# Low queries before value parts, places before scores, and a ScalarE copy of the columns beside the rows: one edit in three stages of a two-layer attention and expert kernel

## The chip, the cores and the metric

The kernel runs on one core of one Trainium2 chip. The metric is device microseconds (us) of one execution; lower is better. Five engines work side by side, each through its own list of instructions in order, and wait for each other on counters (semaphores): TensorE (PE in rows; PEld is its weight load), VectorE (DVE), ScalarE (ACT), GpSimd (POOL) and SyncE (SP, which only issues transfers).

## What is computed

Two layers are applied to 2048 tokens of width 256, each a cross attention over 154 context rows and then a mixture of 8 experts of which each token takes 2. Cut to what matters:

```
x = x + attention0(layernorm(x), ctx, ctx, mask)          # 16 heads of 16, softmax(QK/4 masked) V, then wo
x = x + experts0(layernorm(x))                            # top 2 of 8, silu(x wg) * (x wu), then wd; width 1024
x = x + attention1(layernorm(x), ctx, ctx, side inputs)   # one head of 256, softmax(QK/16 + side) V
x = x + experts1(layernorm(x))                            # top 2 of 8, gelu(x W1a) * (x W1b), then W2; width 512
```

In the second mixture an expert takes at most 640 (token, choice) pairs, in token order; what comes later is dropped.

## The kernel before, in words

The 2048 tokens are 16 tiles of 128, in four groups of 4 tiles (g = 0 to 3). Everything that must be nearly exact is held as a high and a low half-precision part: TensorE multiplies both, and ScalarE usually makes the high part (a cast) and VectorE the low part (value minus high part). The order on each engine is written out by hand, in one function per engine; nothing is scheduled by a program.

**Start of layer one.** TensorE projects keys (`project_keys`) and values (`project_values`, into PSUM banks 6 and 7), turns the first group's normalised tokens and projects its queries. VectorE then makes the key parts (`key_parts`), four `value_parts` (head and remainder parts of the values, for two batches; they release banks 6 and 7 with the signal `kv_done`), the moments and the inverse root of group 1 (`moments`, `scale_and_shift`, whose `a0_nb` lets ScalarE normalise that group), and the low part of the first queries (`q_low(0)`). TensorE's `score_max(0, 1)` waits for that low part. Twelve `score_max` steps fill two pairs of banks in turn and twelve `maximum` steps on VectorE empty them; the query projection of group 1 (`project_q("a0", 1, ...)`) stands among them on TensorE, after step 5, and writes to banks 6 and 7. `negate(0)` and `turn_max(0)` then release the exponentials of group 0.

**Attention of layer two.** Per group g, VectorE adds the attended values to x and takes the routing logits (`attended_rows`), sends the moments to GpSimd (`moments_for_gpsimd`), makes the low part of the next softmax weights (`low_weights`, line 1872), picks the two experts (`choose`), scales the logit difference (`gate_difference`), takes the attention scores of group g + 2 from PSUM and their maxima (`logits(g + 2)`, lines 1854 to 1867), makes the low part of the normalised rows (`low_rows`, line 1901) and computes the place of each row in the experts' lists (`place`, lines 1654 to 1674, signal `r1_slot`). `place(g)` needs the running count from TensorE (`route_positions(g)`, signal `r1_pos_ps`). TensorE's hand-written order there is: weigh the values of group g + 1, count the positions of group g, turn the weights of group g + 2, score the tokens of group g + 3. ScalarE takes the exponentials of group g + 2 as soon as `logits(g + 2)` has given the maxima. GpSimd scatters the rows to DRAM: per group eight indirect transfers (line 631), and before the fifth of them the inverse root of the next group (`scale_and_shift`, lines 608 to 620), which waits for that group's moments.

**The mixtures** (`experts`, once per layer). The sorted rows are read in blocks of 256; a token row of 520 half-precision numbers is high part, low part and, as four 32-bit numbers, the token, two gate weights and the first expert (`TOKEN, SECOND, GAIN, FIRST`). There is one input buffer, `x_raw`. Per block g, TensorE multiplies by the gate and up weights, turns block g + 1 (`turn_block`, line 933, which waits for its load), and multiplies by the down weights; ScalarE applies silu or gelu (line 1267) and casts (line 1271), then issues the load of block g + 2 (`load`, line 1253), then writes the scaled result (line 1280); VectorE multiplies, makes low parts, and in `turned(g + 1)` (lines 1783 to 1790) copies the turned block and works out each row's gate weight from the four trailing numbers, which it reads in `x_raw`, signal `r_carried`; GpSimd adds the result to the sums in DRAM (line 575). ScalarE waits, before the load of block g + 2, for the turning of block g + 1 and for its `r_carried`:

```
act.wait_ge(S(r + "_xbT_ps"), g + 3)
act.wait_ge(S(r + "_carried"), g + 2)
load(g + 2)
split(pairs)
act.wait_ge(S(r + "_down"), g + 2)
wait_counted(act, S(r + "_added"), g + 1)
```

The new weights of a coming expert are converted inside its first block (`high_part` line 1129 on ScalarE, `low_part_of` line 1405 on VectorE); `_added` says that GpSimd's addition of the block before has landed.

Of the kernel before, what the change touches and what calls it, by code (L numbers as in the profile page):

```python
# [16 lines left out]
ALU = mybir.AluOpType  # L17
# [54 lines left out]
def two_layers(nc, a, out):  # L72
    with ExitStack() as ctx:
# [181 lines left out]
        share = sb("share", [P, 2])  # L255
        expert_of = sb("expert_of", [P, AHEAD])
# [235 lines left out]
        def _(pool):  # L492
# [130 lines left out]
            def scatter(l, g):  # L623
                r = l.r
                pool.wait_ge(S(r + "_xp"), g + 1)
                pool.wait_ge(S(r + "_slot"), g + 1)
                for t in range(GT):
                    if l.n == 1 and t == 2 and g + 1 < NG:
                        scale_and_shift("r1", g + 1)
                    for k in range(TOP):  # L630
                        pool.indirect_dma_start(  # L631
                            out=rows, out_offset=bass.IndirectOffsetOnAxis(ap=slot_s[:, g * GT + t, k:k + 1], axis=0),
                            in_=beside_row[g % l.held][:, t, :], in_offset=None, bounds_check=E * REGION - 1,
                            oob_is_err=False).then_inc(S(f"{r}_scattered{g % 2}"), 16)
# [48 lines left out]
        def _(pe):  # L683
# [180 lines left out]
            for n in range(12):  # L864
                score_max(0, n)
                if n == 2:
                    pe.wait_ge(S("k_split"), B)
                    turn("a0", 1, xln, 4, done=3)
                if n == 5:
                    pe.wait_ge(S("kv_done"), 1)  # L870
                    project_q("a0", 1, w_sb["wq"], q_bank(1))
# [237 lines left out]
        def _(act):  # L1109
# [133 lines left out]
            def experts(l):  # L1243
# [10 lines left out]

                def one_block(g, coming=None):
# [6 lines left out]
                    for j in range(pairs + 1):  # L1262
# [5 lines left out]
                        if j:  # L1268
# [3 lines left out]
                            split(j - 1)  # L1272
                    act.wait_ge(S(r + "_xbT_ps"), g + 3)
                    act.wait_ge(S(r + "_carried"), g + 2)
# [25 lines left out]
                load(0)  # L1300
                act.wait_ge(S(r + "_padded"), 16 * (E - 1))
                act.wait_ge(S(r + "_xbT_ps"), 2)
                act.wait_ge(S(r + "_carried"), 1)
# [36 lines left out]
            def tokens_normalised(g):  # L1340

                if g:
                    act.wait_ge(S("r1_xp"), g)
                normalise("r1", g, g + 1)
                act.wait_ge(S("r1_ln"), GT * (g + 1))
                act.copy(xps[g][:, :, 0:D], xln[:, :, :]).then_inc(S("r1_xhi"), 1)
# [14 lines left out]
            gates(L[1], 0)  # L1361
# [4 lines left out]
            gates(L[1], 1)  # L1366
# [3 lines left out]
            gates(L[1], 2)  # L1370
            tokens_normalised(3)
            gates(L[1], 3)
# [4 lines left out]
        def _(dve):  # L1377
# [138 lines left out]
            dve.wait_ge(S("kv_ps"), 2)  # L1516
            for n in range(4):
                value_parts(n // 2, n % 2)
# [198 lines left out]
            q_low(0)  # L1717
            for n in range(12):
                maximum(0, n)
            negate(0)  # L1720
# [54 lines left out]
            def experts(l):  # L1775
# [5 lines left out]
                def turned(g):  # L1781
# [4 lines left out]
                    dve.scalar_tensor_tensor(share[:, :], raw[:, :, FIRST], expert_of[:, bass.ds(g, 1)], raw[:, :, GAIN], ALU.is_equal,  # L1786
                                             ALU.mult).then_inc(S(r + "_share"), 1)
                    dve.tensor_copy(own[:, :, 1].bitcast(I32), raw[:, :, TOKEN].bitcast(I32))
                    wait_counted(dve, S(r + "_share"), g + 2)
                    dve.tensor_tensor(own[:, :, 0], share[:, :], raw[:, :, SECOND], ALU.add).then_inc(S(r + "_carried"), 1)  # L1790

                raw = x_raw[:, :, :].bitcast(F32)
# [105 lines left out]
            def low_rows(g):  # L1898

                dve.wait_ge(S("r1_xhi"), g + 1)  # L1900
                dve.tensor_tensor(xps[g][:, :, D:2 * D], xln[:, :, :], xps[g][:, :, 0:D], ALU.subtract).then_inc(S("r1_xp"), 1)
# [14 lines left out]
            for g in range(NG):  # L1916
# [7 lines left out]
                gate_difference(g)  # L1924
                if g + 2 < NG:
                    logits(g + 2)
                low_rows(g)
                place(L[1], g)
# [47 lines left out]
```

## Time and profile before

| | us |
|---|---|
| median of 3 runs (lowest, highest) | 886.07 (883.26, 892.51) |
| profiled execution, own time | 890.67 |
| its span, first to last instruction | 889.0 |
| mean granted TensorE clock, of full speed | 0.889 |

| stage in the profiled span, us | from | to |
|---|---|---|
| start of layer one, up to the first exponentials | 0 | 54 |
| rest of attention and routing, layer one | 54 | 293 |
| mixture of layer one | 293 | 601 |
| attention and routing, layer two | 601 | 709 |
| mixture of layer two | 709 | 889 |

A row of a timeline reads: start in us, duration in us, engine, line, operation, output<-inputs, shapes, count (x4 is four in a row, with their time in sum), and in brackets how long the engine had been idle and what ended that. A row of stretches gives busy time and count of each engine, then the granted clock, the busy share of the DMA engines and GB/s.

### The profile page before, as it was taken

Reading aid. Unit: us, or ns where it says so; the run is one execution under the profiler, and the core shown is the slowest. Engines: PE = TensorE matmul, PEld = TensorE weight load, DVE = VectorE, ACT = ScalarE, POOL = GpSimd, SP = SyncE. Lnnn points to the kernel's source line nnn. Section 1 sums busy time; section 2 is a strip of 40 time slices with the busy share of each in tenths; the row PEclk is TensorE's granted clock in tenths of the full one; section 3 lists DMA queues with packets and bytes.
Section 4 is the critical chain, followed back from the end, with each engine's and each line's share of the span. In section 5 each row is a group of like instructions: output and inputs, shape, how many; then the busy total and the mean of one; then the engine's idle time right before and its main releaser. Section 6 shows DMA issues by size and latency. Waiting matters only on the chain.

```text
span 889.0 us, 19049 instructions
## 1 busy us (share of the span) xinstructions
PE 700.3 (79%) x6278; PEld 550.1 (62%) x6278; DVE 547.8 (62%) x1322; ACT 403.1 (45%) x720; POOL 302.8 (34%) x306
## 2 busy tenths in 40 slices
PE   5476796989564799999999899996862098898981
PEld 4232454555354688888897798895531087777771
DVE  7768576887836545647556656547696446566441
ACT  1135466576513434646545555442552044546331
POOL 7505301416337422222121131232167414334342
PEclk9689799989776799999999999997875599999996
DMA  4562300601524542536344643425022555464332
GB/s 140 118 141 51 59 2 24 180 24 49 153 81 151 185 129 36 165 51 171 78 126 98 170 112 101 107 39 179 25 101 95 174 170 131 115 147 114 63 55 40
DMA packets 68418, 92.24 MB, mean 104 GB/s; under 512 B 14442, under 2 KB 54435, under 8 KB 68348
## 3 DMA queue, kind: packets, MB, share of 16 engines
q1 hardware_dynamic: 41788, 63.37, 24.1%
q0 software_dynamic: 14592, 16.24, 10.6%
q10 hardware_dynamic: 11968, 11.72, 5.3%
q8 instruction: 42, 0.69, 0.3%
q14 instruction: 28, 0.23, 0.1%
HBM read 64.21 MB, written 29.87 MB: 106 GB/s over the span
## 4 chain that ended last, share of the span: by engine, by line
PE 48%; DVE 18%; issue 11%; ACT 9%; POOL 5%; DMA 5%; ACTq 2%; another core or an unknown queue 1%; DVEq 0%; POOLq 0%; SPq 0%
PE ps L685 45%; POOL rows L631 3%; DVE probs L1726 3%; DVE mx L1591 2%; DMA out_x<-keys,row_to 2%; DVE keys L1804 2%; DMA probs<-rows 2%; ACT probs L1189 1%; ACT probs L1271 1%; ACT expo L1186 1%; DVE keys L1783 1%; ACT probs L1267 1%; PE ps L933 1%; DVE stats L1383 1%; ACTq L1252 1%
## 5 line engine op out<-in xcount | busy, mean ns | idle before, releaser
L1804 DVE TENSOR_TENSOR keys<-probs,ps 128x512 f32<-128x512 f32 x122 | 82.8, 687 | 177.3 <-ACT probs L1267 86.3
L685 PE MATMUL ps<-keys,slot 128*128 128x256 f16 (+1 forms) x1440 | 146.5, 263 | 5.4 <-DVE keys L1783 2.7
L685 PE MATMUL ps<-keys,probs 128*128 128x256 f16 (+1 forms) x1488 | 139.5, 255 | 5.1 <-DVE probs L1405 3.7
L685 PEld LDWEIGHTS ps<-keys,slot 128*128 128x128 f16 x1440 | 127.8, 99 | 22.8 <-issue 5.4
L685 PEld LDWEIGHTS ps<-keys,probs 128*128 128x128 f16 x1488 | 124.2, 98 | 19.0 <-issue 7.2
L575 POOL DMA_INDIRECT attended<-keys,row_to x42 | 67.2, 1601 | 166.0 <-ACT keys L1280 142.2
L1267 ACT ACTIVATE probs<-ps 128x512 f32<-128x512 f32 x122 | 71.4, 598 | 65.9 <-PE ps L685 63.7
L1280 ACT ACTIVATE keys<-ps,carried 128x256 f32<-128x256 f32 x80 | 33.5, 470 | 117.9 <-POOLq L580 41.6
L1809 DVE TENSOR_TENSOR probs<-keys,probs 128x512 f16<-128x512 f32 x122 | 83.3, 688 | 3.6 <-ACT probs L1271 1.9
L1271 ACT CAST probs<-keys 128x512 f16<-128x512 f32 x122 | 74.8, 614 | 22.0 <-DVE keys L1804 21.9
L1726 DVE TENSOR_TENSOR probs<-expo,probs 128x512 f16<-128x512 f32 x80 | 61.1, 775 | 34.1 <-ACT probs L1189 28.2
L685 PE MATMUL ps<-slot,probs 128*128 128x256 f16 x636 | 74.8, 273 | 3.7 <-ACT probs L1271 3.0
L685 PE MATMUL ps<-probs 128*128 128x256 f16 x612 | 72.4, 273 | 4.8 <-ACT probs L1271 4.4
L575 POOL DMA_INDIRECT out_x<-keys,row_to x38 | 58.8, 1548 | 45.6 <-ACT keys L1280 36.6
L1186 ACT ACTIVATE expo<-ps 128x512 f32<-128x512 f32 x80 | 48.2, 602 | 52.8 <-PE ps L685 46.9
L685 PEld LDWEIGHTS ps<-slot,probs 128*128 128x128 f16 x636 | 60.0, 98 | 14.4 <-ACT probs L1271 4.2
L685 PEld LDWEIGHTS ps<-probs 128*128 128x128 f16 x612 | 57.5, 98 | 15.8 <-ACT probs L1271 4.5
L571 POOL COPY row_to<-carried 128x2 int32 x40 | 10.1, 252 | 139.0 <-issue 45.5
L933 PE MATMUL ps<-identh,probs 128*128 128x128 f16 x336 | 26.5, 224 | 36.5 <-DMA probs<-rows 36.5
L685 PE MATMUL ps<-penalties,identb 128*128 128x462 bf16 x96 | 34.8, 363 | 22.2 <-DVE queries L1569 9.4
L1189 ACT CAST probs<-expo 128x512 f16<-128x512 f32 x80 | 49.0, 619 | 0.0
L1405 DVE TENSOR_TENSOR probs<-inbox,probs 128x1024 f16<-128x1024 f32 x36 | 43.6, 1221 | 6.1 <-ACT probs L1129 6.0
(285 smaller groups left out, 1145.7 us busy)
## 6 DMA issues: line engine op xcount, KB each, us to landing
inbox<-in_W SPq DMA_DIRECT2D x24, 512.0 KB, 3.9
probs<-rows ACTq DMA_DIRECT2D x44, 260.0 KB
inbox<-in_wg SPq DMA_DIRECT2D x16, 512.0 KB, 5.2
inbox<-in_wu SPq DMA_DIRECT2D x16, 512.0 KB, 3.7
inbox<-in_wd SPq DMA_DIRECT2D x16, 512.0 KB, 4.2
rows<-zeros SPq DMA_DIRECT2D x16, 260.0 KB
x<-in_x SPq DMA_DIRECT2D x4, 512.0 KB, 6.1
q_out<-queries SPq DMA_DIRECT2D x8, 256.0 KB, 2.1
```

What stands on the lines that cost most here:

```text
L575: pool.indirect_dma_start(out=l.sums, out_offset=bass.IndirectOffsetOnAxis(ap=row_to[:, hf:hf + 1], axis=0), in_=yb[:, hf, :], in_offset=N ...
L685: return pe.matmul(o, l, r, start=start, stop=stop, **kw)
L933: last = pe.transpose(psh[:, 6, part * BLK + hf * P:part * BLK + (hf + 1) * P], x_raw[:, hf, part * P:(part + 1) * P], identh[:, :])
L1186: act.activation(e_ring[:, u % 4, :], ps[:, 4 + u % 2, :], ACT.Exp, scale=float(DK) ** -0.5).then_inc(S("a0_exp"), 1)
L1189: act.copy(p_hi[:, u - 1, :], e_ring[:, (u - 1) % 4, :]).then_inc(S("a0_phi"), 1)
L1267: act.activation(s_act[:, j % 2, :], ps[:, 2 * (j % 2), :], l.act).then_inc(S(r + "_s"), 1)
L1271: act.copy(h_hi[:, 2 * j - 2:2 * j, :].rearrange("p c t -> p (c t)"), h32[:, (j - 1) % 2, :]).then_inc(S(r + "_hh"), 1)
L1280: ins = act.activation(yb[:, hf, :], ps[:, 4 + hf, 0:D], ACT.Identity, scale=carried[:, bass.ds(g, 1), hf, 0:1].rearrange("p b d -> p (b d)"))
L1405: dve.tensor_tensor(w[:, 1, at:at + CH], stage[:, n % STAGES, :], w[:, 0, at:at + CH], ALU.subtract).then_inc(S(f"w_ready{l.n}"), 1)
L1726: dve.tensor_tensor(p_lo[:, u, :], e_ring[:, u % 4, :], p_hi[:, u, :], ALU.subtract).then_inc(S("a0_plo"), 1)
L1804: dve.tensor_tensor(h32[:, j % 2, :], s_act[:, j % 2, :], ps[:, 2 * (j % 2) + 1, :], ALU.mult).then_inc(S(r + "_h32"), 1)
L1809: dve.tensor_tensor(h_lo[:, 2 * j - 2:2 * j, :].rearrange("p c t -> p (c t)"), h32[:, (j - 1) % 2, :], h_hi[:, 2 * j - 2:2 * j, :].rearran ...
```

## The change

It has three parts. (1) At the start of layer one, `q_low(0)` comes before the value parts; the four value parts stand now before maximum 0 and behind maxima 2, 5 and 7, and TensorE's projection of group 1 moves from behind step 5 to behind step 8. (2) In layer two, ScalarE and VectorE make each group's rows in two halves of two tiles, with `gates` between ScalarE's halves, GpSimd waits for a half before the transfers that read it, and `place` and `low_rows` come before `logits(g + 2)`. (3) In both mixtures ScalarE copies the four trailing numbers of block g + 1 to a small tile, `beside_now`, behind its casts of block g; VectorE reads them there, and the load of block g + 2 waits for this copy instead of `r_carried`. The copy itself waits until VectorE has used the block before. Added or moved lines:

```
 def scatter(l, g):
-    pool.wait_ge(S(r + "_xp"), g + 1)
+    if l.n == 0:
+        pool.wait_ge(S(r + "_xp"), g + 1)
     pool.wait_ge(S(r + "_slot"), g + 1)
     for t in range(GT):
+        if l.n == 1 and t % 2 == 0:
+            pool.wait_ge(S(r + "_xp"), 2 * g + t // 2 + 1)
...
-                if n == 5:
+                if n == 8:
                     pe.wait_ge(S("kv_done"), 1)
                     project_q("a0", 1, w_sb["wq"], q_bank(1))
...
+                def keep_beside(g):
+
+                    act.wait_ge(S(r + "_xraw"), g * 16 + 16)
+                    act.wait_ge(S(r + "_carried"), g)
+                    act.copy(beside_now[:, :, :], x_raw[:, :, :].bitcast(F32)[:, :, D:D + 4]).then_inc(S(r + "_beside"), 1)
...
+                    keep_beside(g + 1)
                     act.wait_ge(S(r + "_xbT_ps"), g + 3)
-                    act.wait_ge(S(r + "_carried"), g + 2)
+                    act.wait_ge(S(r + "_beside"), g + 2)
                     load(g + 2)
...
             def tokens_normalised(g):
-                if g:
-                    act.wait_ge(S("r1_xp"), g)
-                normalise("r1", g, g + 1)
-                act.wait_ge(S("r1_ln"), GT * (g + 1))
-                act.copy(xps[g][:, :, 0:D], xln[:, :, :]).then_inc(S("r1_xhi"), 1)
+                for j in range(2):
+                    if g:
+                        act.wait_ge(S("r1_xp"), 2 * g - 1 + j)
+                    half = slice(2 * j, 2 * j + 2)
+                    normalise("r1", g, g + 1, (2 * j, 2 * j + 1))
+                    act.wait_ge(S("r1_ln"), GT * g + 2 * j + 2)
+                    act.copy(xps[g][:, half, 0:D], xln[:, half, :]).then_inc(S("r1_xhi"), 1)
+                    if j == 0:
+                        gates(L[1], g)
...
             key_parts(1)
-            dve.wait_ge(S("kv_ps"), 2)
-            for n in range(4):
-                value_parts(n // 2, n % 2)
             dve.wait_ge(S("ld_x1"), 16)
...
             q_low(0)
+            dve.wait_ge(S("kv_ps"), 2)
+            value_parts(0, 0)
             for n in range(12):
                 maximum(0, n)
+                if n in (2, 5, 7):
+                    part = (2, 5, 7).index(n) + 1
+                    value_parts(part // 2, part % 2)
...
             def low_rows(g):
-                dve.wait_ge(S("r1_xhi"), g + 1)
-                dve.tensor_tensor(xps[g][:, :, D:2 * D], xln[:, :, :], xps[g][:, :, 0:D], ALU.subtract).then_inc(S("r1_xp"), 1)
+                for j in range(2):
+                    half = slice(2 * j, 2 * j + 2)
+                    dve.wait_ge(S("r1_xhi"), 2 * g + j + 1)
+                    dve.tensor_tensor(xps[g][:, half, D:2 * D], xln[:, half, :], xps[g][:, half, 0:D], ALU.subtract).then_inc(S("r1_xp"), 1)
...
                 gate_difference(g)
+                place(L[1], g)
+                low_rows(g)
                 if g + 2 < NG:
                     logits(g + 2)
-                low_rows(g)
-                place(L[1], g)
```

In `turned`, `raw[:, :, FIRST]` and its like become `beside_now[:, :, FIRST - D]`, behind a wait for `r_beside`. The order on the engines, at the two places that matter most (line numbers of the changed kernel run 4 to 17 higher). VectorE in the attention of layer two, group 0, before; `cumb` ends `choose(0)`, `dv` is `gate_difference`, `lg_x` to `mx` is `logits(2)`, `xp<-xln,xp` is `low_rows`, `ohp` begins `place` (its middle left out: from `posk` to `slot_s`), `rd` begins `attended_rows(1)`:

```order
L1646 TENSOR_TENSOR cumb<-cumb,gsum 128x8
L1618 TENSOR_TENSOR dv<-dv,ry_r 128x4
L1854 COPY lg_x<-ps 128x32
L1858 SCALAR_TENSOR_TENSOR expo<-ps,ry_a,keys 128x154 x4
L1865 TENSOR_REDUCE mx<-expo 128x4
L1867 TENSOR_SCALAR mx<-mx 128x4
L1901 TENSOR_TENSOR xp<-xln,xp 128x4x256
L1654 TENSOR_TENSOR ohp<-oh,ps 128x64
L1656 TENSOR_REDUCE posk<-ohp 128x8
...
L1674 TENSOR_TENSOR xp<-dn,xp 128x4
L1878 RECIPROCAL rd<-den 128x4
```

The same place now:

```order
L1656 TENSOR_TENSOR cumb<-cumb,gsum 128x8
L1628 TENSOR_TENSOR dv<-dv,ry_r 128x4
L1664 TENSOR_TENSOR ohp<-oh,ps 128x64
L1666 TENSOR_REDUCE posk<-ohp 128x8
...
L1684 TENSOR_TENSOR xp<-dn,xp 128x4
L1918 TENSOR_TENSOR xp<-xln,xp 128x2x256 x2
L1869 COPY lg_x<-ps 128x32
L1873 SCALAR_TENSOR_TENSOR expo<-ps,ry_a,keys 128x154 x4
L1880 TENSOR_REDUCE mx<-expo 128x4
L1882 TENSOR_SCALAR mx<-mx 128x4
L1893 RECIPROCAL rd<-den 128x4
```

The four steps of `logits(2)` moved from the third row to behind the places and the low rows, which are two halves now.

ScalarE at the end of a block of the mixture, before (`probs<-keys` is the last cast, `TENSOR_LOAD` and `DMA` are the load of block g + 2, `keys<-ps,carried` the scaled result):

```order
L1271 CAST probs<-keys 128x512
L1129 CAST probs<-inbox 128x1024 x2
L1273 REGISTER_ALU
L1274 REGISTER_ALU
L1252 ISA
L1252 TENSOR_LOAD table
L1252 ISA x2
L1253 ISA
L1253 DMA probs<-rows 128x2x260
```

and now:

```order
L1133 CAST probs<-inbox 128x1024 x2
L1261 ISA
L1263 COPY beside_now<-probs 128x8
L1284 REGISTER_ALU
L1285 REGISTER_ALU
L1256 ISA
L1256 TENSOR_LOAD table
L1256 ISA x2
L1257 ISA
L1257 DMA probs<-rows 128x2x260
```

One small copy stands now between the casts and the load; on VectorE nothing moved there.

## Rows read from the trace of the kernel before

**Rows 1.** Stretches (us; PE, PEld, DVE, ACT, POOL busy): mixture one, scatter, mixture two
```profile
307.00:601.00 294.00, 286.59 (x2955) 257.36 (x2953) 172.99 (x285) 148.67 (x244) 68.66 (x59) 0.99 0.44 108
650.00:705.00 55.00, 16.27 (x79) 7.02 (x77) 36.68 (x175) 14.93 (x31) 40.50 (x44) 0.53 0.35 124
719.00:872.00 153.00, 136.72 (x1391) 114.75 (x1388) 87.25 (x168) 72.27 (x127) 60.37 (x53) 1.00 0.50 108
```

**Rows 2.** Timeline of VectorE at the start of layer one
```profile
22.28 0.41 DVE L1493 TENSOR_TENSOR slot<-ps,b_bv 128x256 f32<-128x256 f32 x1
...
28.70 1.40 DVE L1383 BATCH_NORM_STATS2 stats<-x 128x6 f32<-128x256 f32 x4
...
32.80 1.40 DVE L1569 SCALAR_TENSOR_TENSOR queries<-ps,b_bq,queries 128x512 f16<-128x512 f32 x2
...
45.95 2.15 DVE L1591 TENSOR_REDUCE mx<-ps 128x6 f32<-128x924 f32 x2 [3.25 <-PE ps L685]
...
52.33 0.23 DVE L1603 SCALAR_TENSOR_TENSOR nm<-mx,nm 128x64 bf16<-128x64 f32 x1
```

**Rows 3.** Timeline of TensorE at six places of the kernel
```profile
41.50 3.64 PE L685 MATMUL ps<-xT,w_wq 128*128 128x512 f32 x8
...
402.27 5.42 PE L685 MATMUL ps<-keys,slot 128*128 128x256 f16 x48 [1.27 <-DVE keys L1804]
...
616.84 4.69 PE L685 MATMUL ps<-heads,xT 128*128 128x162 f32 x16 [1.10 <-ACT xT L1323]
...
646.33 0.19 PE L685 MATMUL ps<-selb,earlier 128*128 128x32 bf16 x1
...
653.78 6.23 PE L685 MATMUL ps<-probs,queries 128*128 128x264 f16 x24 [2.92 <-DVE queries L1873]
...
661.38 1.12 PE L1058 MATMUL ps<-ident,expo 128*128 128x128 f32 x4 [1.13 <-ACT expo L1329]
```

**Rows 4.** Timeline of ScalarE at a loop's end in layer one, in attention, in mixture two
```profile
397.44 0.84 ACT L1280 ACTIVATE keys<-ps,carried 128x256 f32<-128x256 f32 x2 [3.31 <-issue]
399.43 1.28 ACT L1267 ACT_TABLE_LOAD   x1 [1.14 <-issue]
...
645.77 0.41 ACT L1329 ACTIVATE expo<-expo,mx 128x154 f32<-128x154 f32 x1
...
756.41 0.38 ACTq L1253 DMA_DIRECT2D probs<-rows  x1
757.10 0.84 ACT L1280 ACTIVATE keys<-ps,carried 128x256 f32<-128x256 f32 x2 [3.32 <-POOLq L580]
```

**Rows 5.** Timeline of VectorE in attention of layer two and in mixture two
```profile
642.93 0.18 DVE L1854 COPY lg_x<-ps 128x32 f32<-128x32 f32 x1
...
645.80 1.23 DVE L1901 TENSOR_TENSOR xp<-xln,xp 128x1024 f16<-128x1024 f32 x1 [0.31 <-ACT xp L1346]
646.94 0.21 DVE L1654 TENSOR_TENSOR ohp<-oh,ps 128x64 f32<-128x64 f32 x1
...
648.20 0.17 DVE L1674 TENSOR_TENSOR xp<-dn,xp 128x4 f32<-128x4 f32 x1
...
664.57 0.69 DVE L1872 TENSOR_TENSOR queries<-ps,queries 128x512 f16<-128x512 f32 x1
...
755.47 0.16 DVE L1790 TENSOR_TENSOR carried<-share,probs 128x2 f32 x1 [0.15 <-issue]
```

**Rows 6.** Timeline of GpSimd, scatter of layer two
```profile
649.32 1.11 POOL L631 DMA_INDIRECT rows<-xp,slot_s  x1 [7.80 <-DVE xp L1674]
...
663.28 0.98 POOL L631 DMA_INDIRECT rows<-penalties,slot_s  x1 [0.30 <-issue]
...
668.17 0.23 POOL L608 TENSOR_SCALAR var_p<-mv_r 128x4 f32<-128x4 f32 x1
```

**Rows 7.** Waits from 705 to 889 us: total, times, longest
```profile
ACT keys L1280 <- POOLq L580: 41.6, 11, 4.4
...
PE ps L933 <- DMA probs<-rows: 25.4, 8, 19.2
```

More of the change, by code:

```diff
@@ L255, in two_layers @@
         share = sb("share", [P, 2])
+        beside_now = sb("beside_now", [P, 2, 4])
         expert_of = sb("expert_of", [P, AHEAD])
@@ L1300, in experts @@
                 load(0)
+                act.wait_ge(S(r + "_xraw"), 16)
+                act.copy(beside_now[:, :, :], x_raw[:, :, :].bitcast(F32)[:, :, D:D + 4]).then_inc(S(r + "_beside"), 1)
                 act.wait_ge(S(r + "_padded"), 16 * (E - 1))
                 act.wait_ge(S(r + "_xbT_ps"), 2)
-                act.wait_ge(S(r + "_carried"), 1)
+                act.wait_ge(S(r + "_beside"), 1)
                 load(1)
@@ L1360, in _ @@
             tokens_normalised(0)
-            gates(L[1], 0)
             exponentials(2)
@@ L1365, in _ @@
             tokens_normalised(1)
-            gates(L[1], 1)
             exponentials(3)
@@ L1369, in _ @@
             tokens_normalised(2)
-            gates(L[1], 2)
             tokens_normalised(3)
-            gates(L[1], 3)
             experts(L[1])
@@ L1785, in turned @@
                     wait_counted(dve, S(r + "_share"), g + 1)
-                    dve.scalar_tensor_tensor(share[:, :], raw[:, :, FIRST], expert_of[:, bass.ds(g, 1)], raw[:, :, GAIN], ALU.is_equal,
+                    dve.wait_ge(S(r + "_beside"), g + 1)
+                    dve.scalar_tensor_tensor(share[:, :], beside_now[:, :, FIRST - D], expert_of[:, bass.ds(g, 1)], beside_now[:, :, GAIN - D], ALU.is_equal,
                                              ALU.mult).then_inc(S(r + "_share"), 1)
-                    dve.tensor_copy(own[:, :, 1].bitcast(I32), raw[:, :, TOKEN].bitcast(I32))
+                    dve.tensor_copy(own[:, :, 1].bitcast(I32), beside_now[:, :, TOKEN - D].bitcast(I32))
                     wait_counted(dve, S(r + "_share"), g + 2)
-                    dve.tensor_tensor(own[:, :, 0], share[:, :], raw[:, :, SECOND], ALU.add).then_inc(S(r + "_carried"), 1)
-                raw = x_raw[:, :, :].bitcast(F32)
+                    dve.tensor_tensor(own[:, :, 0], share[:, :], beside_now[:, :, SECOND - D], ALU.add).then_inc(S(r + "_carried"), 1)
                 def low_part(e, slot, n):
```

## The prediction

> **What bounds the kernel now.** I read the stretches first, to see which engine fills which stage, then the timelines of the three places that the change touches, then the list of waits. The two mixtures are TensorE's: it is busy for 286.6 of 294 us in the one and 136.7 of 153 in the other [rows 1]. So a wait there is worth only what TensorE loses to it. In the attention of layer two the picture is another: from 650 to 705 us TensorE is busy for 16 of 55 us, at a granted clock of 0.53. The reader is to see GpSimd's timeline there [rows 6]: from its first scatter at 649.32 on, each step follows on the last with "issue" (0.30) before it, to the last at about 702. The stage ends with GpSimd, and its reserve is small. At 663.28 it starts group 1 and at 668.17 the root for group 2. Whatever delivers late to these two is paid in full. The start of layer one is a chain over VectorE and TensorE: value parts from 22.28, moments from 28.70, the low queries at 32.80, the maxima, and the last negated maximum ends at 52.56 [rows 2].
>
> **Part 1, start of layer one.** The value parts take 28.70 - 22.28 = 6.4 us, the moments and the root 32.80 - 28.70 = 4.1, the low queries 1.4 [rows 2]. The low queries now end at 22.3 + 4.1 + 1.4 = 27.8 instead of 34.2, 6.4 us sooner. But the 6.4 us of value parts are only moved, among the maxima. A maximum takes 2.15 / 2 = 1.08; nine of them (0 to 8) and the four parts are 9.7 + 6.4 = 16.1, so VectorE is through maximum 8 at about 43.9, and the last value part ends one maximum before, at 42.8. TensorE's projection of group 1 (3.64 [rows 3]) waits for exactly that part: 42.8 + 3.6 = 46.4. Behind it stand the scores 9 to 11 (under 1 us each), then three maxima (3.2) and the negation (0.5): 46.4 + 0.8 + 3.7 = 50.9 against 52.6. What hid the projection before was in part VectorE's idle 3.25 [rows 2]; that idle time comes back behind the last value part. Gain 1.7 us. It goes on to the end, as everything later hangs on it. Bounds: a gain of 2.5 if the scores run close, a loss of 1.9 if the projection runs at half the clock after TensorE's waits (3.64 more).
>
> **Part 2, attention of layer two.** Before, VectorE had finished choosing group 0 at 642.93 and went straight into the scores of group 2, 642.93 to 645.49 (the row after waited 0.31 before 645.80), so 2.56 us [rows 5]. Now `place(0)` stands there, and its positions are counted by TensorE only at 646.33 [rows 3], behind the weighing of group 1, which nothing in the change moves. VectorE stands still for 3.7 us, until 646.6. That is an added wait on an engine with the next group's work queued behind it.
>
> Step by step: place 1.43 (646.94 to 648.37), low rows 1.23, say 1.3 in two halves, scores 2.56 [rows 5]: the scores of group 2 end at 646.6 + 1.4 + 1.3 + 2.6 = 651.9 instead of 645.5. Queued behind them: the exponentials (four at 0.41, 1.7 [rows 4]) to 653.7; the turning of the weights and ScalarE's copies, from the turning at 661.38 to the low weights at 664.57 being 3.2 [rows 3, 5], so low weights at 657.0, done at 658.3 (2 x 0.69, less overlap). TensorE meanwhile turns (2.2) and scores group 3, 4.7 at the lower clock [rows 3], to 660.6. The weighing of group 2 took 6.2 at the lower clock; it lies between half of that, 3.1, and 6.2. I take 3.6, since TensorE will have worked for 6.8 us without a pause. So positions of group 1 at 664.5, its place done at 665.9, its first half of low rows at 666.6: GpSimd starts group 1 3.3 us late (663.28).
>
> Then it repeats. Low rows end at 667.2, scores of group 3 at 669.8, exponentials 671.5, low weights 674.7 to 676.0, and only then, in VectorE's order for group 2, the moments (1.4 and 0.4): 677.8. GpSimd wants them after half a group, at 666.6 + 4.9 (663.28 to 668.17) = 671.5; before, it took them at 668.17 [rows 6]. Loss 9.6 us, say 9.5. From there on nothing is late: group 2's place is done at about 683.5, GpSimd comes for it at 686.5. For groups 2 and 3 no scores stand in the way.
>
> The halves gain almost nothing. GpSimd's first scatter waited for the place (`slot`, 648.37), not for the low rows at 647.0; now the place is done at 648.0 and the first half at 648.7. I count 0.
> Bounds of part 2: with both turnings, the scoring and the weighing at the full clock about 5 us less, +5; with the weighing at the lower clock 2.6 more, +12.
>
> **The clock.** The trace shows the lower of the two levels (1.2 against 2.4 GHz) in this stretch, 0.53 granted, after waits of 2.9 us [rows 1, 3]. The Trainium skill ("TensorE: Matmul & The Clock Gate", What's actually happening) says that the slow state is the default and activity releases it. By that rule the longer pauses keep TensorE slow; taken for the weighing too, part 2 costs 12 and not 9.5.
>
> **Part 3, the mixtures.** ScalarE's load of block g + 2 waited for VectorE's `r_carried`, ending at 755.63; the load went out 0.78 later, at 756.41, and the result 0.69 after that, at 757.10, after 3.32 us of idle time, so since 753.8 [rows 4, 5]. Now the load follows on the casts: 753.8, a copy of 8 columns (under the 0.41 of a 154-column step [rows 4]; I take 0.2), 0.8: 754.8, so 1.6 us sooner. Where weights are converted ScalarE is busy until shortly before, and I count about 0.3 there. VectorE's own steps cost the same.
>
> In mixture one TensorE has few gaps. At the ends of ScalarE's loop a table load follows on the late result (397.44 after 3.31 idle, 399.43), and TensorE waits 1.27 at 402.27 [rows 3, 4]; a second such wait, of 1.27 too, stands at 477.32. The result comes 1.4 sooner, bound now by the down product, so both gaps go: 2.5. The last block's result is 1.4 sooner as well, and layer two starts on it: 1.2 after what VectorE's own moments keep back. Sum 3.7; bounds 1.5 and 4.5. The copy itself is hidden under ScalarE's idle 3.3 us per block; uncovered it would be 0.2 per block.
>
> In mixture two TensorE waited for loads for 25.4 us in 8 waits, 19.2 of it the first [rows 7]. The other seven are 6.2 us, under 1.8 each, so 1.6 sooner nearly removes them. Behind each stands the wait for ScalarE's cast, which follows on the result before and moves forward too, but by less where weights are converted. I take three quarters, 4.7; bounds 0.6 and 7.
>
> **Sum.** 890.67 (span 889.0 and 1.7 around it) - 1.7 + 9.5 - 3.7 - 4.7 = 890.1, 0.6 less. The profiled run lies 4.6 above the median; taken from the median, 886.07 - 0.6 = 885.5.
>
> **Rivals.**
> *The moved place costs nothing.* If VectorE's 3.7 us lie beside GpSimd's scatter, only the gains remain, 10.1: 876. For it: VectorE is busy for only 37 of 55 us there [rows 1]. Against it: the exponentials, the weighing and the moments all hang on its order, with GpSimd 1 us behind them.
> *The additions hold mixture two.* ScalarE's result waits for GpSimd's addition of the block before; eleven such waits make 41.6 us [rows 7]. If they are what they seem, an earlier load moves nothing, the gain there is 0.6, and the sum is +3.5, slower: 889.6. It decides where an addition lands later than the load is out. Against it: the result at 757.10 follows on the load by just 0.69, so GpSimd was there already.
> *The slow clock through all of layer two*: part 2 costs 12, sum +1.9: 888.
> *Both, and a slow projection at the start* (3.6 more): +9.6, 895.7.
>
> **Chances.** Forecast 0.45, clock 0.18, additions 0.14, place for nothing 0.15, all against 0.08. The measurement tells about 1% from no change, 8.9 us: faster by more 0.16, within 0.75, slower by more 0.09. The range, 875.5 to 893, takes in the bounds of parts 2 and 3 against each other and the case in which the place costs nothing, and leaves out the last case.
>
> **What would show it.** Right: the first low-query step at about 26.4 and the last negation at 51; VectorE idle 3.6 us before the first `ohp` of layer two, GpSimd waiting once for group 1's place and some 6 us for group 2's moments; the gaps at 402 and 477 gone; 1 to 2 us left of the seven waits for loads. Wrong: GpSimd's scatter still without waits, or the results of mixture two at their old distance.

## The result and the profile after

The changed kernel takes 893.12 us (median of 20 runs, 886.34 to 900.88), the kernel before 883.73 (20 runs). The ratio is 1.0091, 95% interval 1.0075 to 1.0108: some 8 us slower, just outside the range I gave and on its slow side. The two medians lie 9.4 us apart; the ratio counts the fast runs alone (one of the 20 was slow), and its interval, 6.6 to 9.5 us, holds that too. I had forecast no change.

The two profiled executions hide this: after took 890.15 us, 3 below its median, and before 890.67, 7 above its own; the spans are 888.4 and 889.0. What makes up the difference is mostly the stretch up to the first turned block of mixture one, which ends anywhere from 285 to 294 us in the seventeen profiles of this study, with no relation to what was changed that I can see. So I compare stages, not spans. The stages go from the first turned block of mixture one to layer two's first turned token ("mixture one"), from there to the first turned block of mixture two ("attention two"), and to the end ("mixture two"):

| us | up to mixture one | mixture one | attention two | mixture two |
|---|---|---|---|---|
| before | 293.4 | 320.4 | 95.4 | 179.8 |
| after | 288.4 | 312.2 | 102.5 | 185.3 |
| after, a second profile | 291.2 | 314.3 | 99.4 | 183.7 |

Mixture one is shorter, attention two longer, and mixture two, from which I expected 4.7 us less, is 3.9 to 5.5 us longer. The stretches of after that answer to [rows 1] (mixture one, scatter, mixture two; columns as there):

```profile
307.00:596.00 289.00, 284.06 (x2941) 256.16 (x2938) 170.62 (x286) 150.48 (x266) 72.88 (x62) 1.00 0.44 107
640.00:700.00 60.00, 17.54 (x96) 10.32 (x96) 38.59 (x183) 18.57 (x44) 36.40 (x43) 0.56 0.33 116
713.00:872.00 159.00, 137.98 (x1400) 116.23 (x1396) 88.55 (x169) 74.89 (x146) 62.88 (x53) 0.99 0.48 105
```

TensorE's work is the same, but mixture two now holds 138.0 us of it in 159 instead of 136.7 in 153: it waits more. For what, the waits of after from 705 to 889 us say (engine, line, what it waited for, total, times, longest), beside [rows 7]:

```profile
ACT keys L1291 <- POOLq L581: 48.5, 12, 5.4
...
POOL row_to L572 <- DMA out_x<-keys,row_to: 40.6, 11, 5.0
```

and over 705 to 887 us:

```profile
PE ps L937 <- DMA probs<-rows: 2.7, 2, 1.6
```

In the kernel before, over 705 to 889 us, the middle one was:

```profile
POOL row_to L571 <- DMA out_x<-keys,row_to: 32.3, 11, 3.2
```

TensorE's waits for loads behind the first, 6.2 us before, are down to 2.7, as forecast. But GpSimd's eleven waits until an addition has landed grew from 2.9 to 3.7 us each, and the waits of ScalarE's results for that from 41.6 us in 11 to 48.5 in 12. In the chain that ended last the additions' landing now has 8% of the span, before 2%.

In attention two the marks that I had named are there, and two more short waits of GpSimd. VectorE stands still before the first place, GpSimd waits 1.57 us for the moments of group 1, 1.56 for the rows of group 1 and 5.6 for the moments of group 2 (timelines of after, VectorE and GpSimd):

```profile
634.78 0.22 DVE L1664 TENSOR_TENSOR ohp<-oh,ps 128x64 f32<-128x64 f32 x1 [3.98 <-PE ps L689]
```

```profile
637.76 1.11 POOL L635 DMA_INDIRECT rows<-xp,slot_s  x1 [8.46 <-DVE xp L1918]
...
644.30 0.23 POOL L609 TENSOR_SCALAR var_p<-mv_r 128x4 f32<-128x4 f32 x1 [1.57 <-DVE mv_r L1408]
...
653.55 0.97 POOL L635 DMA_INDIRECT rows<-penalties,slot_s  x1 [1.56 <-DVE penalties L1918]
...
663.98 0.23 POOL L609 TENSOR_SCALAR var_p<-mv_r 128x4 f32<-128x4 f32 x1 [5.61 <-DVE mv_r L1408]
```

At the start of layer one the low queries come at 26.95 us, 5.9 sooner than in [rows 2], and yet the negation is late. VectorE (with GpSimd's clearing of a query tile beside it) and TensorE in after:

```profile
26.95 1.40 DVE L1579 SCALAR_TENSOR_TENSOR queries<-ps,b_bq,queries 128x512 f16<-128x512 f32 x2
...
33.26 0.20 DVE L1512 COPY v_rem<-quad_of 128x16 f16<-128x16 f16 x1
...
41.74 1.27 DVE L1512 COPY v_rem<-quad_of 128x16 f16<-128x16 f16 x1
...
50.07 2.15 DVE L1601 TENSOR_REDUCE mx<-ps 128x6 f32<-128x924 f32 x2 [5.50 <-PE ps L689]
...
53.25 0.22 DVE L1613 SCALAR_TENSOR_TENSOR nm<-mx,nm 128x64 bf16<-128x64 f32 x1
```

```profile
41.15 1.80 POOL L553 MEMSET qs<- 128x2048 f32 x1
```

```profile
43.85 5.40 PE L689 MATMUL ps<-xT,w_wq 128*128 128x512 f32 x8 [3.10 <-DVE v_rem L1516]
```

Two things are not as reckoned: the copy of 16 columns takes 1.27 us where its twin takes 0.20, and the projection 5.40 where it took 3.64 [rows 3].

### The profile page after: what moved, and what is told of

It is laid out like the page before. It is cut to its first block, busy times and chain, and to the rows that moved or that the text cites. A ratio compares the mean times of both kernels' runs of the same rounds, so it can differ in the third digit from the quotient of the medians.

```text
span 888.4 us, 19136 instructions
## 1 busy us (share of the span) xinstructions
PE 699.8 (79%) x6266; PEld 555.9 (63%) x6278; DVE 551.2 (62%) x1326; ACT 408.1 (46%) x766; POOL 305.1 (34%) x306
## 4 chain that ended last, share of the span: by engine, by line
PE 48%; DVE 17%; issue 11%; DMA 10%; ACT 7%; POOL 4%; POOLq 1%; ACTq 1%; DVEq 0%
PE ps L689 45%; DMA out_x<-keys,row_to 8%; DVE probs L1741 3%; DVE mx L1601 2%; POOL rows L635 2%; ACT probs L1193 2%; PE ps L937 1%; ACT expo L1190 1%; DVE stats L1396 1%; POOL out_x L576 1%; ACT probs L1133 1%; DMA probs<-rows 1%; ACT keys L1291 1%; DVE expo L1873 1%; DVE queries L1579 0%
## 5 line engine op out<-in xcount | busy, mean ns | idle before, releaser
L689 PE MATMUL ps<-keys,probs 128*128 128x256 f16 (+1 forms) x1488 | 137.6, 254 | 4.6 <-DVE probs L1418 3.5
L572 POOL COPY row_to<-carried 128x2 int32 x40 | 14.0, 350 | 149.1 <-issue 48.6
```

Of the source, the lines that this page charges most:

```text
L689: return pe.matmul(o, l, r, start=start, stop=stop, **kw)
```

## The experiments

Each kernel was timed against the kernel before on its own chip, so ratios compare and medians don't.

### Each part alone

The first of these has the diff's edits to `q_low`, `value_parts` and `project_q`; the second those to `scatter`, `tokens_normalised`, `low_rows` and `place`; the third those to `keep_beside`, `load` and `turned`.

> The kernel before with part 1 alone (low queries ahead of the value parts, projection of group 1 behind step 8). Theory: the profile after shows the projection at 5.40 us instead of 3.64 and the last negation 0.9 us later, so part 1 is a small loss: ratio 1.000 to 1.002, some +1 us, the last negation at about 53.4. Rival (my prediction's term): a gain of 1.7 us, ratio 0.998, last negation at about 51.

> The kernel before with part 2 alone (row halves and places ahead of the scores in layer two). Theory: the chain over GpSimd's waits costs what the profile after shows, +7 us (stage from the first turn of layer two to the first turn of mixture two 102.5 instead of 95.4 us), ratio 1.007 to 1.009. Rival: the later scatter also takes the whole loss of mixture two with it (by another phase of the weight loads), then +12 us, ratio 1.014, and mixture two at 185 instead of 180 us with the load where it was.

> The kernel before with part 3 alone, in both mixtures (ScalarE's copy, the load waits for it). Theory: the earlier load falls on GpSimd's additions in mixture two, which land 4.2 us after their issue instead of 3.0; mixture two 185 us instead of 180 (+5), mixture one 4 to 8 us shorter, so between -3 and +1 us, ratio 0.997 to 1.001. Rival (the prediction's term): both mixtures gain, -8 us, ratio 0.991, the profile's loss in mixture two coming from elsewhere.

| | ratio (interval) | mixture one | attention two | mixture two |
|---|---|---|---|---|
| part 1 alone | 1.0012 (0.9995 to 1.0029) | 320.9 | 97.1 | 181.3 |
| part 2 alone | 1.0039 (1.0015 to 1.0062) | 320.8 | 100.8 | 179.9 |
| part 3 alone | 1.0004 (0.9975 to 1.0034) | 315.5 | 95.9 | 184.3 |

The stage effects stay with their parts. Part 2 leaves mixture two alone, so that rival falls, but it costs 5.4 us in its stage and not the 7 that I had read off the profile after. Part 3 gains 4.9 us in mixture one and loses 4.5 in mixture two, to no net effect. Part 1 ends its negation at 53.0 and doesn't gain.

### The parts together again

> The changed kernel as it is, on the chip that runs the three below, so that the parts can be added up against it. On another chip the three parts alone came to 1.0012, 1.0039 and 1.0004. If the parts add (theory), their sum is 1.0055; if the earlier load and the later scatter hurt each other (rival), the whole is at 1.008 or more, as in the first measurement (1.0091), and its mixture two is over 1 us longer than with part 3 alone (184.3).

1.0074 (1.0047 to 1.0102). The interval holds both the product of the three parts, 1.0055, and the rival's 1.008, so the ratio doesn't decide. Mixture two is at 183.7, not longer than with part 3 alone, so I see no interaction.

### Part 3 in mixture one alone

```
-                    act.wait_ge(S(r + "_carried"), g + 2)
+                    if l.n == 0:
+                        keep_beside(g + 1)
+                    act.wait_ge(S(r + ("_beside" if l.n == 0 else "_carried")), g + 2)
```

> Part 3 in the first mixture alone; mixture two as before. Theory: in mixture one TensorE sets the end and additions have slack (GpSimd waits for results 130 us there), so the 4.9 us of the profile with part 3 alone stay: ratio 0.993 to 0.996, mixture two at 180 us. Rival: the 4.9 us are chance between profiles and the ratio is 0.998 to 1.002.

0.9946 (0.9924 to 0.9967): faster, with mixture one at 315.0 us and mixture two at 179.4. TensorE's waits there from 287.9 to 603 us:

```profile
PE ps L934 <- issue: 10.7, 1, 10.7
PE ps L1040 <- DMA x<-attended: 6.1, 1, 6.1
PE ps L686 <- DVE probs L1417: 3.5, 1, 3.5
PE ps L686 <- DVE keys L1795: 0.9, 1, 0.9
```

In the kernel before, from 293 to 614 us, the same list was:

```profile
PE ps L933 <- DMA probs<-rows: 11.2, 1, 11.2
PE ps L1039 <- DMA x<-attended: 7.6, 1, 7.6
PE ps L685 <- DVE probs L1405: 3.7, 1, 3.7
PE ps L685 <- DVE keys L1804: 2.5, 2, 1.3
PE ps L685 <- ACT probs L1271: 1.0, 5, 0.2
PE ps L685 <- DVE keys L1783: 0.9, 1, 0.9
```

The two gaps of 1.27 are gone (2.5), and the last wait fell from 7.6 to 6.1: together 4.0. The five short waits for casts (1.0) are no part of the gain, though they are missing here: three other kernels with the copy have them, and four without it don't. The stage is 315.1 us long in the mean of the eight profiles with the copy and 319.9 in the nine without, 4.8 less, but the two groups touch (312.2 to 316.8, and 316.8 to 322.7). TensorE's idle time in the stage tells them apart: 10.3 to 11.8 us with the copy, 14.6 to 16.4 without, 4.5 less in the mean.

### When the load goes out in mixture two

Three kernels move only that. The first two are part 3 alone, but in layer two with

```
+                    if l.n == 1:
+                        act.wait_ge(S(r + "_down"), g + 2)
                     load(g + 2)
```

or with `load(g + 2)` behind `wait_counted(act, S(r + "_added"), g + 1)`. The third is the kernel before with a second load of the same size, into a tile `dump` that nothing reads, issued by ScalarE behind its casts (and behind the landing of the `dump` load before).

> Part 3 in both mixtures, but in layer two the load of block g + 2 waits for the down product of block g too (about 0.7 to 1 us later than with part 3 alone, and still ahead of ScalarE's wait for the addition, so no result waits for the load to be issued). Theory (load and addition share the DMA engines): GpSimd's eleven waits for landing fall from 3.65 us each towards 2.95, and mixture two from 184.3 towards 180 to 182. Rival (the ring is longer for another reason, such as ScalarE's order): mixture two stays at 184 and the waits at 3.6.

> As the run with part 3 alone, but in layer two the load of block g + 2 goes out behind ScalarE's wait for the addition of the block before, so that it does not run while that addition lands. Theory (the load and the additions share the DMA engines): additions land as in the kernel before, about 3 us after their issue, and mixture two is back at 179 to 181 us, 4 to 6 us less than with part 3 alone. Rival (not the load's time but something else of the change holds the ring): the landings stay long and mixture two at 185 us, within 1 us of part 3 alone; second rival: the later load brings TensorE's waits for loads back and costs as much as it gives, mixture two at 183 or more with short landings.

> The kernel before, and in layer two ScalarE issues, behind its casts, a second load of the same size (block g again) into a tile that nobody reads; the real load stays where it was. Theory (a load that runs while an addition lands makes it land later): GpSimd's waits for landing rise from 2.95 to 3.6 us or more each, though no data waits for this load, and mixture two gets 4 to 8 us longer, part of that ScalarE's time to issue it. Rival (transfers don't meet; the early load hurts by another order of waits): the landings stay at 2.9 to 3.1 us, and mixture two gets longer by the issue alone, up to 0.7 us in each of the six blocks that convert weights.

| | ratio (interval) | landing, us each | mixture two |
|---|---|---|---|
| before | 1 | 2.94 | 179.8 |
| part 3 alone | 1.0004 (0.9975 to 1.0034) | 3.65 | 184.3 |
| load behind the down product | 0.9959 (0.9940 to 0.9979) | 3.14 | 179.7 |
| load behind the wait for the addition | 1.0081 (1.0052 to 1.0111) | 3.12 | 192.4 |
| before, with a second load | 1.0109 (1.0086 to 1.0132) | 3.40 | 189.7 |

The landing column is the wait row divided by its eleven waits; for part 3 alone, for the load behind the down product, and for the second load (705 to 887 us):

```profile
POOL row_to L572 <- DMA out_x<-keys,row_to: 40.1, 11, 4.2
```

```profile
POOL row_to L572 <- DMA out_x<-keys,row_to: 34.5, 11, 4.4
```

```profile
POOL row_to L572 <- DMA out_x<-keys,row_to: 37.4, 11, 3.9
```

What costs sits at the results of the blocks of 128 rows, whose casts are through early (an expert's last block, of half the width). At five of the six, GpSimd's waits are 2.77 to 3.12 us before, 3.75 to 4.24 with part 3 alone (5.3 us more in sum, of 7.8 in all eleven) and 2.77 to 2.89 with the load behind the down product; at the sixth they are 2.96, 3.23 and 2.89. In that last kernel the first, third and fifth of the eleven waits stay long (3.94, 4.36 and 3.36), and yet mixture two is as short as before; these three are the only ones beside which packets of a weight load run. ScalarE and GpSimd at such a result with part 3 alone:

```profile
733.07 0.39 ACTq L1254 DMA_DIRECT2D probs<-rows  x1
737.06 0.84 ACT L1288 ACTIVATE keys<-ps,carried 128x256 f32<-128x256 f32 x2 [4.96 <-POOLq L581]
```

```profile
732.10 1.54 POOL L576 DMA_INDIRECT out_x<-keys,row_to  x1 [0.30 <-issue]
737.47 0.19 POOL L572 COPY row_to<-carried 128x2 int32 x1 [3.83 <-DMA out_x<-keys,row_to]
```

and with the load behind the down product:

```profile
728.30 0.39 ACTq L1254 DMA_DIRECT2D probs<-rows  x1
730.20 0.84 ACT L1291 ACTIVATE keys<-ps,carried 128x256 f32<-128x256 f32 x2 [3.94 <-POOLq L581]
```

```profile
726.27 1.54 POOL L576 DMA_INDIRECT out_x<-keys,row_to  x1 [0.30 <-issue]
730.61 0.19 POOL L572 COPY row_to<-carried 128x2 int32 x1 [2.81 <-DMA out_x<-keys,row_to]
```

In the first, the load goes out 4.0 us ahead of the result, while GpSimd is still issuing the second half of the addition (732.10 to 733.64); the addition lands 1.0 us later than in the second, where the load goes out 1.9 us ahead of the result, 0.5 us after GpSimd has issued the second half. The second load, whose data nothing uses, lengthens the landings too, from 2.94 to 3.40 us on average (3.6 or more were expected; mixture two grew by more than the 4 to 8 expected). So it is the load's traffic, and not another order of waits, that makes additions land later.

The kept traces also hold start, size and queue of every single packet, which the rows above don't list. They show how. With part 3 alone, at each of those five, 143 to 194 of the load's 256 packets (1040 bytes each) start ahead of the first 1 KB packet of the addition's second half, which starts 1.5 to 1.8 us after GpSimd has issued it. In the kernel before, and with the load behind the down product, none does, and that packet starts after 0.6 us. The second half queues behind the load. The Trainium skill ("DMA: Bandwidth & Descriptors", Queues, rings and completion order) says that each DMA engine takes turns between the queues that have work for it and finishes a whole packet, typically 9 to 17 descriptors, before it switches. By that rule a load would pass in one piece: its 256 entries of the trace are 16 for each of 16 engines, an estimate, as the trace names no engine. The order in the trace agrees with it; that it is the reason isn't shown.

How much of the 9.9 us that the second load adds to mixture two is landing, and how much ScalarE's time to issue it, stays open. With the load behind the wait for the addition, additions land in 3.12 us, but every result then waits until the load is issued, TensorE waits for loads again (14.3 us in 11 waits), and it is the slowest of the mixtures. So the second rival of that run was right. The right place lies between, and the kernel before already had its load there.

### The result in halves

```
-                    wait_counted(pool, S(r + "_y"), g + 2)
                     for hf in range(2):
+                        wait_counted(pool, S(r + "_y"), g * 2 + (2 + hf))
```

with ScalarE signalling `_y` after each half.

> The kernel before, with one difference: ScalarE signals each half of the scaled result, and GpSimd issues the addition of the first half on that signal, 0.42 us sooner than behind both. Theory (the ring result, addition, landed, result sets mixture two): each ring of 16 full blocks gets 0.4 us shorter, and mixture two 3 to 6 us, ratio 0.994 to 0.997. Rival (TensorE sets mixture two, the ring only looks late): under 1 us, ratio 0.999 to 1.001.

1.0009 (0.9991 to 1.0026): nothing, the rival's number, and in the full blocks for its reason. In eleven of nineteen blocks GpSimd did use the earlier signal: from the start of the result to the addition it is 1.35 us where it was 1.72. Mixture two is no shorter for it. Before (its result is the last row of [rows 4]), and then with halves (ScalarE, GpSimd):

```profile
758.82 1.55 POOL L575 DMA_INDIRECT out_x<-keys,row_to  x1 [1.51 <-ACT keys L1280]
```

```profile
749.43 0.84 ACT L1280 ACTIVATE keys<-ps,carried 128x256 f32<-128x256 f32 x2 [3.32 <-POOLq L580]
...
750.79 1.55 POOL L575 DMA_INDIRECT out_x<-keys,row_to  x1 [1.27 <-ACT keys L1280]
```

At the other eight, those of blocks of 128 rows among them, the gain is 0.1 us or less, as the addition there follows on GpSimd's own small copy, and that on the landing. Before, and then with halves:

```profile
740.17 0.19 POOL L571 COPY row_to<-carried 128x2 int32 x1 [2.77 <-DMA out_x<-keys,row_to]
741.49 1.55 POOL L575 DMA_INDIRECT out_x<-keys,row_to  x1 [1.14 <-ACT keys L1280]
```

```profile
732.49 0.18 POOL L571 COPY row_to<-carried 128x2 int32 x1 [2.82 <-DMA out_x<-keys,row_to]
733.72 1.55 POOL L575 DMA_INDIRECT out_x<-keys,row_to  x1 [1.04 <-ACT keys L1280]
```

From copy to addition it is 1.32 us the one time and 1.23 the other. So in a full block the ring has time to spare, and in a block of 128 rows it is GpSimd and the landing, with ScalarE's wait of 4 us as its shadow. That fits with a later landing being paid, at the blocks of 128 rows, and an earlier result bringing nothing.

### Part 2 taken apart

Halves alone is part 2 without the move of `place` and `low_rows`. The other is part 2 with `route_positions(L[1], 0)` ahead of `weigh_tokens(1)`.

> Only the row halves of layer two (ScalarE, VectorE and GpSimd's two waits), with places and low rows behind the scores as in the kernel before. Theory: the halves are worth nothing and the moved places are all of part 2's cost: ratio 0.999 to 1.001, stage from the first turn of layer two to the first of mixture two at 95 to 96 us. Rival: the halves themselves cost (twice the instructions on VectorE and ScalarE), ratio 1.002 to 1.004 and a stage of 98.

> Part 2 alone, but TensorE counts the positions of group 0 ahead of weighing group 1 (in PSUM bank 4, which is free there) and not behind it. Theory (the moved place costs because it waits for positions that stand behind the weighing on TensorE): VectorE's idle time before the first place falls from 3.66 us to under 1, GpSimd's first scatter and everything behind it comes 3 us sooner, its waits for group 1 (2.35) stay, and of the 5 to 6 us that part 2 adds to the stage 2 to 3 are left (98 instead of 100.8 us; ratio 1.000 to 1.002 against 1.0039). Rival (the scores of group 2 are late by place and low rows anyway, whatever the wait): the stage stays at 100 to 101 us.

Halves alone: 0.9997 (0.9974 to 1.0021), attention two at 95.5 us. So the halves are free within the interval, and the moved places are the cost. Positions first: 1.0057 (1.0030 to 1.0083), attention two at 99.6. The wait is gone and the loss is not. VectorE and GpSimd of that run:

```profile
640.47 0.22 DVE L1658 TENSOR_TENSOR ohp<-oh,ps 128x64 f32<-128x64 f32 x1 [0.39 <-PE ps L688]
...
659.28 0.22 DVE L1658 TENSOR_TENSOR ohp<-oh,ps 128x64 f32<-128x64 f32 x1 [4.01 <-PE ps L688]
```

```profile
644.29 1.11 POOL L634 DMA_INDIRECT rows<-xp,slot_s  x1 [5.72 <-DVE xp L1907]
...
662.17 0.97 POOL L634 DMA_INDIRECT rows<-penalties,slot_s  x1 [3.65 <-DVE penalties L1907]
...
672.61 0.23 POOL L608 TENSOR_SCALAR var_p<-mv_r 128x4 f32<-128x4 f32 x1 [5.63 <-DVE mv_r L1399]
```

GpSimd's waits are 3.65 and 5.63 instead of 2.35 and 5.62 with part 2 alone. The theory of this run is mostly wrong: 1.2 us of the stage came back, not 2 to 3 (the ratio is no smaller than part 2's, as this profile is also 2 to 3 us longer in the two mixtures, which it doesn't touch). The order itself costs: the scores of group 2 start 33.4 us into the stage, against 35.7 with part 2 alone and 29.4 before, so that 4.0 of the 6.3 us stay although the first wait is gone. That much the rival had right. With the place ahead, the scores of group 3 hang on the positions of group 1, these stand behind the weighing of group 2, and that hangs on the scores of group 2: a ring. From the scores of group 2 to those of group 3 it takes 17.9 us here and 16.6 with part 2 alone, against 13.6 in the kernel before and 13.96 from one group's first scatter to the next in [rows 6]. The scores in their old place didn't hang on the positions. That the ring sets these times is read from the order; no run opened it.

### Part 1 taken apart

> Part 1 alone, but with TensorE's projection of group 1 behind step 11 instead of 8. Theory: what cost part 1 its gain is the projection in the middle of the scores, 3.1 us of TensorE idle and 5.3 us of projection while VectorE sits idle for 5.4; behind the last score it lies beside the last three maxima. Last negation at about 48 instead of 52.8, the first exponential group 4 us sooner, and if that goes on to the end, ratio 0.995 to 0.997 (part 1 alone: 1.0012). Rival: the time is given back in the attention of layer one, where TensorE and VectorE are filled anyway, ratio 0.999 to 1.001 with the negation still early.

> Part 1 alone, with GpSimd's clearing of the second query tile (1.80 us, at 40.8) held back until the last value part is done. Theory (VectorE's copy v_rem<-quad_of, 1.27 to 1.66 us instead of 0.20 in three profiles with part 1, is held by that clearing, since it ends each time 0.06 us behind it): the copy takes 0.19 to 0.20 us and the last value part ends 1.1 us sooner, at about 42.4. Rival (the copy is slow for another reason, its place behind the maxima for one): it stays over 1 us. The whole time is no test, 1 us is too little.

The projection behind step 11: 0.9994 (0.9972 to 1.0016). The negation starts at 48.38, 4 us sooner, but TensorE's next step now waits behind the projection, and the first scores of group 0 start at 52.53 instead of 53.88: 1.35 us, too little to measure. (In the ten profiles with the old start they come at 53.0 to 55.0, 54.1 in the mean.)

The clearing held back behind the last value part (a single run, for its timeline). VectorE, GpSimd and TensorE:

```profile
41.73 0.19 DVE L1501 COPY v_rem<-quad_of 128x16 f16<-128x16 f16 x1
...
50.47 0.22 DVE L1602 SCALAR_TENSOR_TENSOR nm<-mx,nm 128x64 bf16<-128x64 f32 x1
```

```profile
42.78 1.80 POOL L554 MEMSET qs<- 128x2048 f32 x1 [1.74 <-DVE v_rem L1505]
```

```profile
42.77 3.70 PE L687 MATMUL ps<-xT,w_wq 128*128 128x512 f32 x8 [2.02 <-DVE v_rem L1505]
```

The copy takes 0.19 us, the projection starts at 42.77 and takes 3.70, and the negation is through at 50.7. The last run below repeats all three. The kernel before already showed the clash, in a row I hadn't read:

```profile
23.03 1.84 POOL L552 MEMSET slot<- 128x2048 f32 x1
```

```profile
24.42 0.51 DVE L1499 COPY v_rem<-quad_of 128x16 f16<-128x16 f16 x1
27.80 0.19 DVE L1499 COPY v_rem<-quad_of 128x16 f16<-128x16 f16 x1
```

The clearing ends at 24.87 and the copy that meets it at 24.93; in after they end at 42.95 and 43.01. The Trainium skill ("SBUF — State Buffer", SBUF: two separate sides) says that VectorE and GpSimd share a pair of memory ports, which whichever starts first holds for its whole instruction while the other stands. It limits this to some VectorE instructions, such as a copy in a mode that uses both ports. Both pairs of rows agree, with 0.06 us between the ends; in which mode the copy ran, no row says.

### The parts that pay, together

> The parts that should pay, together: part 1 with the projection behind step 11, and part 3 in mixture one alone; layer two as before. Part 3 in mixture one alone gave 0.9946. Theory: with the 4 us of the start 0.990 to 0.992. Rival (the start's gain is given back): 0.994 to 0.996.

> Part 1 with GpSimd's second clearing behind the last value part, and part 3 in mixture one alone; attention and mixture of layer two as before. Theory: the first scores of group 0 start at about 51.9 instead of 53.9 (2.0 us), mixture one is 4.8 us shorter, mixture two stays at 179 to 181: together 6.8 of 885, ratio 0.992. Rival (the start's gain does not reach the end, as the 1.35 us with the projection behind step 11 did not show): 0.9946, as with part 3 in mixture one alone.

0.9926 (0.9898 to 0.9955) with the projection behind step 11, 0.9940 (0.9912 to 0.9969) with the mended start. Both beat the kernel before, by 0.6 to 0.7%. Neither is told apart from part 3 in mixture one alone, 0.9946, so that the start's 1.4 to 2 us reach the end isn't shown.

## Why the prediction was wrong

Taking for each stage the mean of the profiles with and without its part, the terms are +0.6, +5.5, -4.8 and +4.2: 5.5 us more, where I had 0.6 less. The second measurement, 1.0074, holds 5.5 in its interval (4.2 to 9.0 us); the first, 6.6 to 9.5 us, leaves 1 us or more that I can't place.

- **Part 1, forecast -1.7 us; +0.4, +0.8 and +1.1 at the first scores of three profiles, against the one of before.** Against the mean of the ten with the old start it is +0.6, within their scatter. Order and sum were right: once the clearing is out of the way, the last value part ends at 42.7 and the negation at 50.7, where the text says 42.8 and 50.9. What failed is the step "the four parts are 6.4": a moved copy was costed by its duration in its old place, and GpSimd's clearing, which stands in the new one, was not looked for. The projection at a lower granted clock (0.74 from 43.5 to 50 us, 1.00 before) was within my bounds, as the loss is.
- **Part 2, forecast +9.5; +5.5 over three profiles against 95.4 in thirteen.** The mechanism was right step by step: VectorE idle for 3.7 (3.66 with part 2 alone), the weighing of group 2 at 3.6 (3.59, where it had taken 6.23 at the lower clock in [rows 3]), group 1 of the scatter 3.3 late (2.9 into the stage), GpSimd's waits together 9.6 (1.57, 2.35 and 5.62 us, 9.5). What was mis-sized is "whatever delivers late to these two is paid in full", and with it the reading of GpSimd's rows. Of its 32 scatter issues in the kernel before, five take 1.6 to 2.0 us and not 0.97; in the kernels with part 2 there are only two above 1.2. That gives back 2.8 of the 9.5 and leaves 6.7, beside the 6.2 by which the scatter, first issue to last, got longer (52.1 to 58.3 with part 2 alone). Also, taking the first wait away gave back 1.2 us of the stage only; the order costs the rest.
- **Part 3 in mixture one, forecast -3.7; -4.8.** Right: the two gaps went (2.5 as reckoned), and the last wait gave 1.5 where I had 1.2.
- **Part 3 in mixture two, forecast -4.7; +4.2** (184.4 in the three profiles with the early load, 180.2 in the eleven whose load in layer two is the one of before). This is the step that failed. "Removing 1.6 us before each load removes seven waits of 6.2 us" came true at the waits, and was the wrong account: I treated the load as free traffic. Sent sooner, it runs while the addition before it lands, its packets ahead of those of the addition's second half. I had the rival of the additions with the right place and a price of 0.6 gained at best; it gave no thought to the additions getting slower themselves, so even the worst case of the range had no loss here. The argument against that rival, "GpSimd was there already" at 757.10, was no argument: there the result followed GpSimd's signal, as the row [rows 4] says in its own bracket.

The 9 us between forecast and outcome in mixture two are more than the whole loss; the 4 us too much in part 2 covered part of it.

## What to carry to other kernels

A transfer that goes out sooner isn't only a wait that ends sooner: ask which other transfer it now runs beside, and whether a ring closes over that one. Before an instruction is moved on VectorE, look at what GpSimd does at the new place, and look for its twin among the rows with an odd duration. And where a step is moved ahead of another in a chain per group, reckon the ring of one group, not the first wait: a wait taken away showed here only the next one.

## What the runs showed that I had not expected

- An addition to DRAM that lands in 2.94 us (mean of 11) took 3.75 to 4.24 in five cases where ScalarE issued a 260 KB load 0.5 to 0.6 us before GpSimd had issued the second half, and 2.77 to 2.89 in the same five where the load went out 0.5 us after.
- A copy of 128x16 half-precision numbers takes 0.19 us alone and 0.51, 1.27, 1.31, 1.62, 1.66 and 1.72 beside a clearing by GpSimd, and ends 0.05 or 0.06 us behind it each time.
- The projection took 3.70 us where TensorE had been idle for 2.02 us before it, and 5.28, 5.40 and 5.12 us where it had been idle for 3.20, 3.10 and 3.55.
- GpSimd's indirect scatter is issued in 0.97 us, but in the kernel before, without pauses, five of 32 took 1.6 to 1.96, and with the pauses of part 2 only two took over 1.2 (1.45 and 1.99). So GpSimd's waits weren't paid in full. What makes the five long wasn't tried.
